# A macaron block on one core: the recurrence's batch written out in a new order on four engines

## The reference, cut to what matters

```python
x = x + _L0_attn_ref(_layernorm(x, axis=-1), ...)
# in it: r, k, v, g are projections of mixes of x and x shifted by one token; 16 heads of 8 channels;
# 512 tokens in 4 chunks of T = 128
def step(s, chunk):
    rr, kk, vv = chunk
    att = einsum('bhik,bhjk->bhij', rr, kk) * w_mat
    out = att @ vv + einsum('bhik,bhkv->bhiv', rr, s) * wb
    s_new = ws * s + einsum('bhjk,bhjv->bhkv', kk * wk, vv)
    return (s_new, out)
# then per token and head: group norm of out / 8 with ln_w, ln_b; times silu(g); times W_o.T
```

## Time and profile before

| what | value |
|---|---|
| median of 3 runs | 1745.0 us (1743.45 to 1745.64) |
| the profiled execution | 1737.57 us |
| its span, first to last instruction | 1735.8 us |
| TensorE busy / VectorE / ScalarE / GpSimd | 94% / 68% / 55% / 51% |
| mean granted TensorE clock | 0.984 of full |

### The profile page before, as it was taken

How to read it: one execution, slowest core, us unless ns; L and a number is a source line. 1 busy time by engine, 2 the same in 40 slices (tenths; PEclk the granted TensorE clock), 3 DMA queues, 4 the chain that set the end, 5 groups by cost and what they waited for, 6 DMA issues and landing times. The chain is left out here.

```text
span 1735.8 us, 44222 instructions
## 1 busy us (share of the span) xinstructions
PE 1627.9 (94%) x15774; PEld 955.8 (55%) x15774; DVE 1180.4 (68%) x2655; ACT 946.7 (55%) x1844; POOL 889.8 (51%) x756
## 2 busy tenths in 40 slices
PE   6899999999999888899999999999899998999888
PEld 4566666666666555566666666666544333344344
DVE  5865665666766777666666566666787877788566
ACT  5655555555554333455555555566434766677623
POOL 2665665755743566675575576574541322222232
PEclk9999999999999999999999999999998999999999
DMA  4200000000010222000000000000001111111000
GB/s 148 69 28 1 0 0 0 0 0 0 2 25 14 62 50 49 2 2 2 1 0 0 0 0 0 0 2 2 1 1 40 36 26 27 26 27 26 2 14 37
DMA packets 23835, 31.31 MB, mean 18 GB/s; under 512 B 3722, under 2 KB 20234, under 8 KB 23572
## 3 DMA queue, kind: packets, MB, share of 16 engines
q1 hardware_dynamic: 23700, 29.49, 6.5%
HBM read 10.47 MB, written 2.10 MB: 7 GB/s over the span
## 5 line engine op out<-in xcount | busy, mean ns | idle before, releaser
L550 POOL TENSOR_TENSOR scratch<-scratch 128x512 f16<-128x512 f32 x379 | 440.0, 1161 | 418.6 <-ACT scratch L726 418.4
L1198 DVE SCALAR_TENSOR_TENSOR scratch<-psum,scratch 128x512 f32<-128x512 f32 x512 | 353.2, 690 | 311.6 <-ACT scratch L721 184.7
L726 ACT ACTIVATE scratch<-scratch 128x512 f16<-128x512 f32 x512 | 322.4, 630 | 433.7 <-DVE scratch L1198 433.6
L1726 PE MATMUL psum<-ffn_down_hi,scratch 128*128 128x128 f16 x2048 | 369.3, 219 | 1.7 <-POOL scratch L550 1.7
L1728 PE MATMUL psum<-ffn_down_hi,scratch 128*128 128x128 f16 x2048 | 369.2, 219 | 0.0
L1727 PE MATMUL psum<-ffn_down_lo,scratch 128*128 128x128 f16 x2048 | 369.2, 219 | 0.0
L721 ACT ACTIVATE scratch<-psum 128x512 f32<-128x512 f32 x512 | 296.8, 580 | 0.3 <-PE psum L1690 0.2
L1588 DVE TENSOR_REDUCE scratch<-psum 128x2 f32<-128x1024 f32 (+3 forms) x256 | 202.5, 821 | 61.8 <-PE psum L2150 58.7
L1726 PEld LDWEIGHTS psum<-ffn_down_hi,scratch 128*128 128x128 f16 x2048 | 200.3, 98 | 59.8 <-POOL scratch L550 3.2
L1727 PEld LDWEIGHTS psum<-ffn_down_lo,scratch 128*128 128x128 f16 x2048 | 200.4, 98 | 56.0
L1688 PE MATMUL psum<-x_hi,ffn_up_hi 128*128 (+1 forms) x512 | 195.3, 381 | 8.2 <-DVE scratch L1198 8.1
(11 more groups left out here) (222 smaller groups left out, 2612.4 us busy)
## 6 DMA issues: line engine op xcount, KB each, us to landing
scratch<-scratch SPq DMA_DIRECT2D x96, 128.0 KB, 2.7
raw<-in_ffn_w_dram SPq DMA_DIRECT2D x8, 768.0 KB, 4.4
ffn_up_hi<-scratch SPq DMA_DIRECT2D x32, 128.0 KB, 2.7
x_tok<-in_x_dram SPq DMA_DIRECT2D x8, 256.0 KB, 6.5
out_dram<-x_tok SPq DMA_DIRECT2D x8, 256.0 KB, 2.0
raw<-in_lin_dram SPq DMA_DIRECT2D x1, 1092.0 KB
con_sb<-in_con_dram SPq DMA_DIRECT2D x1, 410.5 KB, 4.7
con_sb<-in_con_dram SPq DMA_DIRECT2D x1, 320.5 KB, 3.4
```

Of the source, the lines that this page charges most:

```text
L550: pool.tensor_tensor(h_lo[r], h32[r], h_hi[r], ALU.subtract).then_inc(s_plo, 1)
L726: act.activation(h_hi[k % HSLOTS], h32[k % HSLOTS], ACT.Copy).then_inc(s_hhi, 1)
L1198: dve.scalar_tensor_tensor(h32[k % HSLOTS], bank(5 + k % 2), W_DOWN, gate_act[k % 2], ALU.mult, ALU.mult).then_inc(s_h, 1)
L1726: pe.matmul(dst, h_hi[r][:, cols], hi, start=k % FC == 0 and n == 0, stop=False, skip_group_check=True)
```

## The change

The loops over n in `body` are gone on ScalarE, VectorE and TensorE; the same calls are written out once for a batch, in another order. `group_norm` is now `normed` and `gated`, with `weigh_keys` of the next batch's chunk 1 between them. The conditions for the first and last batches are the same. GpSimd's code and SP's are unchanged. Below are the new bodies; the loops that they replace are in the code above.

```diff
@@ scalar, rwkv: body(b, before, prep, more)
-                    for n in range(SUB):
...
+                    u = SUB * b
+                    if before:
+                        y_copy(b - 1)
+                        squares(b - 1)
+                    values(u + 2, 2)
+                    if more:
+                        r_high(b + 1)
+                        r_low(b + 1)
+                    values(u + 3, 3)
+                    if prep:
+                        prep_xT(n0 + SUB * b + LEAD, (b + 2) % NB, PROJ)
+                    if more:
+                        values(u + 4, 0)
+                    if before:
+                        gate_silu(b - 1)
+                        widen_rstd(b - 1)
+                    if b + 2 < NB:
+                        k_high(b + 2)
+                    if more:
+                        values(u + 5, 1)
+                    if b + 2 < NB:
+                        k_low(b + 2)
+                    if before and more:
+                        y_high(b - 1)
@@ vector, rwkv
-                def group_norm(b):
-
+                def normed(b):
                     dve.wait_ge(s_grb, b + 1)
...
                     dve.scalar_tensor_tensor(y_n, y_c, col_("ln_w"), bank(at), ALU.mult, ALU.mult).then_inc(s_yn, 1)
+
+                def gated(b):
+                    y_n, y_g, silu_g = gn_set(b)[0], gn_set(b)[1], gn_set(b)[3]
                     dve.wait_ge(s_yn, b + 1)
                     dve.wait_ge(s_sg, b + 1)
                     dve.scalar_tensor_tensor(y_g, y_n, col_("ln_b"), silu_g, ALU.add, ALU.mult).then_inc(s_yg, 1)
@@ vector, rwkv: body(b, before, prep, more)
-                    for n in range(SUB):
...
+                    u = SUB * b
+                    new_state(b, 1)
+                    weigh(u + 1, 1)
+                    weigh_keys(u + 2, 2)
+                    if before:
+                        variance(b - 1)
+                    if static and b == 0:
+                        prep_bn(n0 + LEAD, LEAD)
+                        prep_aggr(n0 + LEAD, True)
+                    if more:
+                        r_weighed(b + 1)
+                    new_state(b, 2)
+                    if before == 2:
+                        add(b - 2)
+                    weigh(u + 2, 2)
+                    if stats:
+                        if static and b + 3 >= NB:
+                            dve.wait_ge(s_rout, b + 5 - NB)
+                        prep_bn(n0 + SUB * b + SUB * 3, SUB * bx)
+                    if prep:
+                        prep_low(n0 + SUB * b + LEAD, (b + 2) % NB if static else b + 2, PROJ)
+                    if more:
+                        weigh_keys(u + 4, 0)
+                    if stats:
+                        dve.wait_ge(s_xn, n0 + SUB * b + SUB * 3)
+                    weigh(u + 3, 3)
+                    if stats:
+                        prep_aggr(n0 + SUB * b + SUB * 3, True)
+                    if more:
+                        new_state(b + 1, 0)
+                        weigh(u + 4, 0)
+                    if before:
+                        normed(b - 1)
+                    if more:
+                        weigh_keys(u + 5, 1)
+                    if before:
+                        gated(b - 1)
@@ tensor, rwkv: body(b, odd, before, prep, more)
-                    for n in range(SUB):
...
+                    u = SUB * b
+                    scores(u + 1, b, 1, odd)
+                    state_product(u + 1, b, 1)
...
+                    if more:
+                        r_proj(b + 1)
+                    keys_values(u + 2, b, 2)
+                    if before:
+                        gn_var(b - 1)
+                    if before == 2:
+                        out_proj(b - 2)
+                    state_product(u + 2, b, 2)
+                    outputs(u, b, 0)
+                    scores(u + 2, b, 2, odd)
+                    if more:
+                        r_rest(b + 1)
+                    keys_values(u + 3, b, 3)
+                    if before:
+                        g_proj(b - 1)
+                    if prep:
+                        pe.wait_ge(s_rlo, b + (2 if more else 1))
+                        prep_transpose(n0 + SUB * b + LEAD, PROJ)
+                    if more:
+                        keys_values(u + 4, b + 1, 0)
+                    scores(u + 3, b, 3, odd)
+                    outputs(u + 1, b, 1)
+                    outputs(u + 2, b, 2)
+                    if more:
+                        state_product(u + 4, b + 1, 0)
+                    if keys:
+                        k_proj(b + 2)
+                    if more:
+                        scores(u + 4, b + 1, 0, 1 - odd)
+                    outputs(u + 3, b, 3)
+                    if before:
+                        gn_rstd(b - 1)
+                    if more:
+                        keys_values(u + 5, b + 1, 1)
+                    if keys:
+                        k_rest(b + 2)
```

More of the change, by code:

```diff
@@ L1482, in variance @@
                     dve.tensor_scalar(gn_set(b)[4], bank(at, a, a + SUB * H), GN_EPS, None, ALU.add).then_inc(s_gvar, 1)
-                def group_norm(b):
+                def normed(b):
                     dve.wait_ge(s_grb, b + 1)
-                    y_n, y_c, _, silu_g, _, _, at, _ = gn_set(b)
-                    y_g = y_c
+                    y_n, y_c, at = gn_set(b)[0], gn_set(b)[1], gn_set(b)[6]
                     if not (isinstance(b, int) and b == 0):
@@ L1513, in rwkv @@
                     if late == 6:
-                        group_norm(NB - 1)
+                        normed(NB - 1)
+                        gated(NB - 1)
                     if late == 12:
@@ L2049, in body @@
                     keys = not isinstance(b, int) or b + 2 < NB
-                    for n in range(SUB):
[L2051 to L2060, removed]
-                            r_proj(b + 1)
-                        if n == 1 and more:
-                            r_rest(b + 1)
-                        if more or n < SUB - 2:
-                            keys_values(u + 2, b2, n2)
-                        if n == 0 and before:
-                            gn_var(b - 1)
-                        if n == 0 and before == 2:
-                            out_proj(b - 2)
-                        if n == 1 and prep:
-                            pe.wait_ge(s_rlo, b + (2 if more else 1))
-                            prep_transpose(n0 + SUB * b + LEAD, PROJ)
-                        if n == 2 and before:
-                            g_proj(b - 1)
-                        if n == 3 and keys:
-                            k_proj(b + 2)
-                        if n == 3 and before:
-                            gn_rstd(b - 1)
-                        outputs(u, b, n)
-                        if n == 3 and keys:
-                            k_rest(b + 2)
@@ new lines, in body @@
+                    u = SUB * b
+                    scores(u + 1, b, 1, odd)
+                    state_product(u + 1, b, 1)
+                    if isinstance(b, int) and b == 0:
+                        begin(pe, ph["i"])
+                    if more:
[6 more added lines that the diff above has]
+                    state_product(u + 2, b, 2)
```

## The result

The changed kernel takes 1716.13 us, the median of 4 runs (1714.69 to 1719.8), where the kernel before takes 1744.42 beside it (4 runs, 1743.45 to 1745.64): ratio 0.9841, 95% interval 0.9823 to 0.9858, so 28.3 us less. Its profiled execution took 1716.8 us (span 1715.1) where that of before took 1737.57: 20.8 less.

A forecast was written before the change was run, and what follows sets the result against it. The bound was taken as a chain that changes engine, no engine filling a batch. Recurrence 22.6 plus batch 7's 1.5, minus 1 for neighbours, gave gain 23: 1737.57 to 1714.5, 1722 on the median's scale; range 1716 to 1733.

The forecast's parts named there:

- The replay: One middle batch worked through in the new order from start-to-start times: period 17.5 us, seven distances summing to 121.5 against 144.06.
- y_high(6) 1.5 us earlier: End of batch 7: y_copy(7) and squares(7) no longer hold up y_high(6), which starts at 717.1 instead of 718.68; 1.5 us.
- The allowance for new neighbours: TensorE: changed neighbour pairs cost 0 to 0.11 us at some six places; 0.15 a batch taken, minus 1 in all.
- The power's loop: Loop from gn_var through GpSimd's power, widening, gn_rstd and norm back to gn_var: 16.8 us, deciding only if lengthened from 17.5.
- Slack 0.5 us: At the norm: possible at 19.2 us, while VectorE comes to it at 19.7, so the power was taken as hidden.
- 0.67 + 0.43 + 0.44 + 1.29 + 0.66 back to gn_var: Last hops of the loop, from the norm through weigh_keys, state_product and TensorE to gn_var, within its 16.8 us.
- Collision: Rival: gate_low starts first on GpSimd, making new_state(b,1) 0.85 us late in each of six batches, 5.1 us; 1727, chance 0.15.
- Floor: Rival: queued weight loads and shorter slots make up the hops, 16.8 us a batch, 4 to 5 us more gained; 1718, chance 0.1.
- Half: Rival: missed TensorE waits lengthen the batch one for one; with 1.7 us missed, 19.2 a batch, gain 12; 1733, chance 0.12.
- Norm first: Rival: normed ahead of weigh_keys(b+1,1) on VectorE holds the batch if the loop lengthens; at 23 us a batch 1752, chance 0.04.
- No change: Rival: the feed-forward, filled by TensorE, gives the whole gain back; chance 0.02.
- 7.4 above it: Scale term: the shown median 1745.0 lies 7.4 us above the profiled execution 1737.57, taking forecast 1714.5 to 1722.

The follow-up runs named there:

- g_short: Changed kernel with four of g_proj's six matmuls (the products with low halves) left out in batches 0 to 6: 1717.01 us, ratio 0.985.
- pow_long: Changed kernel with one more power on 4 columns on GpSimd ahead of the group norm's power, each batch 0 to 6: 1725.26 us, ratio 0.99.
- norm_whole: Changed kernel with gated right behind normed, ahead of weigh_keys of chunk 1, so the group norm is in one part: 1723.02 us, ratio 0.9879.
- edge: Changed kernel with keys_values(b+1,1) ahead of outputs(b,3) and gn_rstd, values ahead of k_high, weigh_keys ahead of the undivided norm: 1719.02 us, ratio 0.9857.
- after_again: The changed kernel measured once more, nothing altered, against the kernel before: 1717.46 us, ratio 0.9855.
- before_again: The kernel before measured once more, nothing altered, 10 runs: 1743.33 us, ratio to its other copy 0.9992.
- widen_first: Kernel before with only widen_rstd moved ahead of k_high on ScalarE: 1731.61 us, ratio 0.994.
- outputs_early: Changed kernel with outputs(b,1) ahead of scores(b,3) on TensorE: 1717.95 us, ratio 0.9846.

## Why the prediction was right

**The mechanism.** The replay gave 17.5 us for each of batches 2 to 5 and 121.5 for the sum; the trace has 17.41, 17.42, 17.22 and 17.48, and 121.90. Its single steps stand where it put them. Counted from weigh(b,0) at 657.47, the norm comes at 2.20 (2.21), state_product(b,1) at 3.41 (3.31), new_state at 3.92 (3.85), weigh(b,1) at 4.51 (4.45), and widen_rstd 17.61 after the weigh(b,0) before (17.8; it is 17.82 in the two batches before). One hop was shorter: from scores to weigh(b+1,0) 0.46 us in this batch and 0.54 in the ones before, not 0.62, which is about what the batches are under 17.5. TensorE waits 0.24 us before state_product(b,1), where about 0.6 was forecast, since scores(b,1) was done only at 660.6, and in the batches before it waits 0.15; VectorE waits 0.88 and 0.34 (about 1 and 0.7). "y_high(6) 1.5 us earlier" measured 1.57: 695.46 - 557.29 = 138.17 against 161.90 before, less the 22.16 of the batches. From weigh(0,1) to the feed-forward's third gate product the traces have 167.04 and 143.29: 23.75 us, where the steps had 24.1.

**The allowance for new neighbours** (minus 1) was too much by half or more, and what was used of it went elsewhere: the batches sum to 121.90, 0.4 above the replay without it. Batch 0 took 17.70 (17.4) and batch 1 17.46 (17.0: to leave out out_proj didn't shorten it, since TensorE waits 0.51 us for weigh_keys before its state_product(1,2)); batches 2 to 5 are 0.5 under the replay together, and batch 6 took 17.21 (17.1).

**The power's loop** was put at 16.8, with "Slack 0.5 us". The loop is 17.35 in batches 1 to 3 and 17.21 in batch 5. The step that was short is "0.67 + 0.43 + 0.44 + 1.29 + 0.66 back to gn_var": it follows the norm to weigh_keys and on through TensorE, but the variance stands on VectorE behind weigh(b,1), and in batch 5 weigh_keys also waits for `values` behind gn_rstd. g_short and pow_long show it. It changed nothing in the time, because TensorE was the longer by 0.07 us; that it was is luck and not the working. It is why removing 0.87 us of TensorE's work brought 0.07.

**The rivals.** Collision: none in the changed kernel (0.35 us sixteen times), and norm_whole shows that the mechanism and the order that decides it are real: with gate_low 0.4 to 0.6 us ahead it happens in every batch. The changed kernel stands 0.41 on the right side at new_state(6,1) (0.4 in the replay), but only 0.28 at new_state(3,1) and (4,1). Floor (16.8): no; even with less work on TensorE it stopped at 17.35, by the loop. Half: no; nothing on TensorE waits beyond 0.24 in batches 2 to 5. Norm first: the norm never waited (gn_rstd at 658.77 and the hop of 0.66 make 659.43, VectorE came to it at 659.67), though norm_whole and edge show how little was left. No change: the feed-forward kept the gain; attention's first reduction (L1588, now L1599) comes 23.1 us earlier and its last 22.8.

**The size.** 1722 was 6 us high, and 1716.13 stands only 0.1 inside the lower end of the range (1716), so that it stayed in is in part luck. One term is the reason: "7.4 above it", the distance from the profiled execution to the median. The steps gave 1714.5 for an execution like the profiled one, whose granted clock was 0.984. The changed kernel took 1715.46 and 1713.58 us in its two executions at 0.984. But before's medians come from executions at lower clocks. Forty of them in later jobs have a mean clock of 0.980, and go by it: 1739.75 us on average at 0.983 (3 executions), 1743.38 at 0.980 (4), 1747.36 at 0.977 (3). The changed kernel's eight have 0.982 on average: 1715.78 at 0.983 (2) and 1717.9 at 0.980 (3). At equal clock the gain is therefore 24.0 (0.983) and 25.5 (0.980), close to the 23 to 24 of the steps. The rest of 28.3 would be a little less clock for the old order, and chance in medians of four (the next measurement, after_again, gives 25.3); how much each is, no run tells. A possible cause is visible in one trace: in before_again the clock fell to 1.2 GHz inside batch 3, behind idle time that the new order doesn't have. That is one of three traces of the old order, widen_first among them, and none of eleven of the new. In batch 0 it fell in two of the three and in three of the eleven, so that place tells the two orders apart little. That this is what the timed executions of before did is argued from their clocks, not shown: they have no trace.

## What to carry to other kernels

With queues in order and nothing added or removed, replay one period by start-to-start times from the trace; it came within 0.3 us of each middle batch here, and within 0.1 of three of the four, and it also says which neighbour pairs will be on the edge. Follow every loop through each queue that it passes, also where it seems to have slack: this one was 0.5 us longer than its hops alone. First look for an instruction whose input has long been ready behind one that isn't urgent: two lines swapped on ScalarE were 11 of 25 us. Take the difference forecast from one execution to the median only with the granted clock beside both.

## What the runs showed of the hardware that I had not expected

Two bounds 0.07 us apart hid each other in the middle batches: four matmuls less gave 0.07 us a batch, half the power gave nothing, both gave 0.5. Two VectorE and GpSimd instructions collide or don't by a few tenths of a us of order: new_state's second half took 0.66 to 0.86 us when gate_low had started 0.4 to 0.6 ahead, 1.20 when it had started 0.04 ahead, and 0.35 when it started first. The same half kept its 0.35 inside the power of 10.5 us, which also has two inputs in SBUF, with one exception: in pow_long it took 0.46 to 0.49 in four batches, where the short power ended 0.05 to 0.09 us after its start and the long one began 0.01 to 0.05 us after it:

```profile
614.87 0.49 DVE L1476 SCALAR_TENSOR_TENSOR scratch<-scratch 128x128 f32<-128x128 f32 x1
```
```profile
614.92 10.53 POOL L647 TENSOR_TENSOR scratch<-scratch,neg_half 128x64 f32<-128x64 f32 x1
```

The Trainium skill, "SBUF — State Buffer", section "Who interferes with whom", has a VectorE instruction with two SBUF inputs contend with a GpSimd one that reads SBUF, by an exclusive lock, with the order of issue deciding who is blocked. The runs agree for gate_low in nine cases (one each in before, before_again and widen_first, six in norm_whole): in all nine the half ended 0.14 or 0.15 us after gate_low. For the long power they don't: no half that started inside it was held, while the four of pow_long were lengthened by 0.11 to 0.14 us at the turn from one power to the next; which of the two did it is open.

And the granted clock of one program differs from execution to execution: 0.83, 0.50 and 0.82 in batch 7 of one trace of the changed kernel and 1.00 in the other. In outputs_early it was 0.50 from 692 to 700; it fell while TensorE waited 2.25 us for widen_rstd before gn_rstd, which put the feed-forward's third gate product 2.4 us late (145.73 against 143.29).
